# Block 0 of a fused cross-attention and FP4 feed-forward kernel: the ring place in the down weights' room given up for four more bias sums, and the last four pairs of tiles projected in quarters

## What is computed

```
xn   = layernorm(x)
h    = tanh(text_proj[t] + feat_proj[row] + b)     # for every row, every one of 77 tokens, 512 wide
rho  = sum over the 512 of h * w                   # one score for each row and token
att  = softmax over tokens; two gates per row, tanh(att . u) and tanh(att . v)
x    = x + gate_w * xn + gate_b
x    = x + fp4_linear(silu(fp4_linear(xn2, w_gate)) * fp4_linear(xn2, w_up), w_down)
```

## Time and profile before

| | before |
|---|---|
| median of 3 runs | 1538.8 us (1537.33 to 1539.91) |
| the profiled execution's own time | 1539.24 us |
| its span | 1537.4 us |
| busy share of PE, ACT, DVE, POOL | 93%, 88%, 75%, 16% |
| chain that ended last: PE, ACT, DVE | 52%, 27%, 17% |

### The profile page before, as it was taken

The page is one execution under the profiler, slowest core; times in us unless marked ns, Lnnn a source line. Parts: engine busy times, 40 slices in busy tenths (PEclk is TensorE's granted clock), DMA queues, the critical chain, the costliest instruction groups (busy, mean ns, idle before and its releaser), DMA issues.

```text
span 1537.4 us, 24122 instructions
## 1 busy us (share of the span) xinstructions
PE 1432.1 (93%) x9752; PEld 647.7 (42%) x9752; DVE 1157.2 (75%) x1783; ACT 1359.6 (88%) x1249; POOL 248.7 (16%) x389
## 2 busy tenths in 40 slices
PE   7988889856999999999999999989999999999998
PEld 4444444411333333334444444434444444555564
DVE  4699997944586666759666776698877787898887
ACT  5999989999999999999999999999999999433321
POOL 0122222200111010111011111011101111312211
PEclk9999999988999999999999999999999999999999
DMA  5133332320011111201111111112111111123332
GB/s 159 42 83 83 83 82 75 95 65 8 8 26 41 40 27 41 40 15 40 41 40 40 41 33 37 36 40 40 40 41 41 40 41 40 40 59 73 80 69 62
DMA packets 181557, 77.91 MB, mean 51 GB/s; under 512 B 163627, under 2 KB 165675, under 8 KB 181445
## 3 DMA queue, kind: packets, MB, share of 16 engines
q1 hardware_dynamic: 180224, 75.00, 21.0%
q10 hardware_dynamic: 1221, 1.36, 0.3%
HBM read 27.85 MB, written 8.39 MB: 24 GB/s over the span
## 4 chain that ended last, share of the span: by engine, by line
PE 52%; ACT 27%; DVE 17%; issue 2%; DMA 1%; POOL 1%; SPq 0%; ACTq 0%; DVEq 0%; POOLq 0%
PE rho L809 19%; ACT hring L628 17%; PE dn L906 10%; PE gu1g L892 5%; PE gu0g L892 5%; PE gu1u L892 5%; PE gu0u L892 5%; ACT hring L623 4%; DVE featT L985 2%; ACT wd_room L628 2%; DVE work L1019 2%; ACT featT L623 1%; ACT featT L628 1%; DVE work L1040 1%; DVE work L1039 1%
## 5 line engine op out<-in xcount | busy, mean ns | idle before, releaser
L628 ACT ACTIVATE hring<-featT,bias 128x1024 f32<-128x1024 f32 x688 | 729.2, 1156 | 2.6 <-PE rho L809 2.5
L809 PE MATMUL rho<-hring,wslide 128*32 128x512 f32 x3776 | 459.0, 611 | 61.5 <-ACT hring L628 52.4
L809 PEld LDWEIGHTS rho<-hring,wslide 128*32 128x32 f32 x3776 | 105.5, 111 | 338.6 <-issue 191.7
L628 ACT ACTIVATE featT<-featT,bias 128x1024 f32<-128x1024 f32 x220 | 236.3, 1178 | 2.2 <-PE rho L809 2.2
L906 PE MATMUL dn<-wd_room,turned 128*128 128x512 f16 x1023 | 230.6, 380 | 0.2 <-DMA turned<-work 0.2
L490 POOL TENSOR_SCALAR split_t<-sm 128x32 f32<-128x32 f32 (+4 forms) x82 | 19.7, 240 | 1178.1 <-DVE sm L1008 1178.1
L623 ACT ACTIVATE hring<-featT 128x4096 f32<-128x4096 f32 x57 | 207.5, 3640 | 0.4 <-DVE featT L985 0.4
L985 DVE TENSOR_SCALAR featT<-featT,bias 128x1024 f32<-128x1024 f32 x256 | 175.5, 750 | 11.9 <-ACT hring L623 7.6
L1309 DVE TENSOR_TENSOR work<-sg,gu1u 128x352 f32<-128x352 f32 x64 | 33.3, 521 | 173.9 <-ACT sg L661 173.1
L906 PEld LDWEIGHTS dn<-wd_room,turned 128*128 128x128 f16 x1023 | 96.4, 98 | 145.2 <-issue 36.0
L809 PE MATMUL rho<-featT,wslide 128*32 128x512 f32 x1056 | 126.4, 596 | 5.4 <-ACT featT L628 3.1
(11 more groups left out here) (228 smaller groups left out, 1578.5 us busy)
## 6 DMA issues: line engine op xcount, KB each, us to landing
xt<-in_x SPq DMA_DIRECT2D x32, 256.0 KB, 2.8
out<-xt SPq DMA_DIRECT2D x32, 256.0 KB, 2.3
work<-in_x SPq DMA_DIRECT2D x8, 512.0 KB, 4.1
xt<-in_x SPq DMA_DIRECT2D x6, 512.0 KB, 4.3
xt<-in_L_ffn_w_gate SPq DMA_DIRECT2D x11, 256.0 KB, 2.7
xt<-in_L_ffn_w_up SPq DMA_DIRECT2D x11, 256.0 KB, 3.0
work<-in_L_ffn_w_down SPq DMA_DIRECT2D x2, 704.0 KB, 5.1
xt<-in_L_ffn_w_down SPq DMA_DIRECT2D x2, 704.0 KB, 4.1
```

The costliest lines, as they stand in the source:

```text
L628: act.activation(slot[s][:, g, :], featT[:, e, ROW0[k]:ROW0[k] + rows], ACT.Tanh, bias=bias[:, e, base + tok:base + tok + 1]).then_inc(tan ...
L809: last = pe.matmul(rho[SLOTW * g:SLOTW * g + SLOTW, hf * 512:hf * 512 + 512], wslide[:, e, SLOTW - 1 - r:2 * SLOTW - 1 - r], slot[s][:, g, ...
```

## The change

It does three things in block 0.

- The ring has two places from quad 43 to quad 76: place 3 is given up. Its bytes stay the room of the bias sums.
- Four more quads are summed: 49, 53, 58 and 62, twelve in all. Round w = 8 of DVE's list gets two sums (quads 49 and 53), and two more stand behind `copy_pair(10)` (quad 58) and behind `down_weights(0)` (quad 62). SP now starts its transposes into `wd_room` when ACT has finished tanh 62.
- Pairs 8 to 11 (w = 9 to 12) are projected in quarters of 8 profile instructions behind the quads at + 1 to at + 4: 49 to 52, 54 to 57, 58 to 61 and 63 to 66. The transposes of pair 11 come behind the last quarter of pair 9, at quad 57.

```diff
--- before.py
+++ after.py
@@ -69,9 +69,9 @@
 
     assert BLOCKS == (1024,) * 4
     DEPTH = (2, 2, 3, 3)
-    HEAD_PLACE = [4] * 43 + [None] * 2 + [3] * 16 + [None] * (QPB - 61)
-    SUM_ROUNDS = (0, 2, 4, 6)
-    FIRST_SUMS = (13, 17, 22, 26, 31, 35, 40, 44)
+    HEAD_PLACE = [4] * 43 + [None] * (QPB - 43)
+    SUM_ROUNDS = (0, 2, 4, 6, 8)
+    FIRST_SUMS = (13, 17, 22, 26, 31, 35, 40, 44, 49, 53, 58, 62)
     ring_pos, ring_prev = [], []
     last_user = [-1] * 5
     for k in range(NBLK):
@@ -81,7 +81,7 @@
             ring_pos.append(at)
             ring_prev.append(last_user[at] if last_user[at] >= 0 else None)
             last_user[at] = QPB * k + q
-    LAST_IN_WD, LAST_IN_FEATURES = last_user[3:]
+    LAST_IN_FEATURES = last_user[4]
 
     G_COST, D_COST = 3.6, 2.4
     slots = {}
@@ -400,7 +400,7 @@
             sp.wait_ge(pair_turned, PAIRS)
             passed()
             load_wd(1)
-            sp.wait_ge(quad_used, LAST_IN_WD + 1)
+            sp.wait_ge(tanh_ready, GRP * (FIRST_SUMS[-1] + 1))
             for r in range(KC):
                 sp.wait_ge(wdq_ready, r + 1)
                 passed()
@@ -614,10 +614,6 @@
                     act.wait_ge(pair_ready, PAIRS)
                 if s == 2 and ring_prev[n] is None:
                     act.wait_ge(tanh_ready, GRP * n)
-                if s == 3 and ring_prev[n] is None:
-                    act.wait_ge(feat_filled, len(FEAT))
-                    act.wait_ge(text_filled, KC)
-                    act.wait_ge(tanh_ready, GRP * (FIRST_SUMS[-1] + 1))
                 if n in SUMMED:
                     act.wait_ge(summed, GRP * (SUMMED[n] + 1))
                     act.activation(slot[s], rooms[room_of[n]], ACT.Tanh).then_inc(tanh_ready, GRP)
@@ -824,19 +820,19 @@
                         last = pe.transpose((tr, dn)[t][:, k * P:k * P + P], xpair[p % 2][:, t, k * P:k * P + P], idf[:])
                 last.then_inc(pair_turned, 1)
 
-            def project_pair(p, half):
+            def project_pair(p, chunks):
 
                 pe.wait_ge(pair_copied, p + 1)
                 if p < 2:
                     pe.wait_ge(uv_ready, 1)
                 else:
                     pe.wait_ge(pair_ready, p - 1)
-                for e in (2 * half, 2 * half + 1):
+                for e in chunks:
                     for k in range(KC):
-                        last = pe.matmul(gu[p % 2][half][:, (e % 2) * 256:(e % 2) * 256 + 256],
+                        last = pe.matmul(gu[p % 2][e // 2][:, (e % 2) * 256:(e % 2) * 256 + 256],
                                          Wf[:, k, e * P:e * P + P], xnT2[p % 2][:, k, :],
                                          start=(k == 0), stop=(k == KC - 1))
-                if half == 1:
+                if KC - 1 in chunks:
                     last.then_inc(pair_projected, 1)
 
             for n in range(QPB):
@@ -859,10 +855,9 @@
                     at = 8 + 9 * w // 2
                     if n == at and w < PAIRS:
                         turn_pair(w)
-                    if n == at + 1 and w > 0:
-                        project_pair(w - 1, 0)
-                    if n == at + 2 and w > 0:
-                        project_pair(w - 1, 1)
+                    per = 1 if w > 8 else 2
+                    if w > 0 and n > at and per * (n - at) <= KC:
+                        project_pair(w - 1, range(per * (n - at - 1), per * (n - at)))
 
             def softmax_transposes(k, hf):
                 pe.wait_ge(rho_drained, k + 1)
@@ -1203,8 +1198,10 @@
                 if w in SUM_ROUNDS:
                     sum_quad()
             copy_pair(NC - 1)
+            sum_quad()
             features_pair(NC - 2)
             down_weights(0)
+            sum_quad()
             copy_pair(NC)
             features_pair(NC - 1)
             down_weights(1)
```

## The result

| | before | changed kernel |
|---|---|---|
| median of 7 runs each | 1538.99 us | 1543.88 us (1540.86 to 1545.48) |
| ratio | | 1.0029, 95% interval 1.0019 to 1.0039 |
| the profiled execution and its span | 1539.24, 1537.4 | 1540.86, 1539.1 |
| eleven further runs, beside 33 of before | 1538.54 | 1542.52 (1540.79 to 1545.32), ratio 1.0023 (1.0014 to 1.0032) |

The changed kernel is slower, by 0.2 to 0.4%. The forecast of 1541.7 has the sign and the place; the median of the first runs is 2.2 us above it and that of the further ones 0.8, both inside the range. One run of before (1563.72) was a disturbed one and is left out of the ratio.

The account below looks back on a forecast made before the run. ACT was taken to bound block 0: quad 63 starts 3.5 us later, less 0.58 before quad 67, so 2.9 us later; on a median of 1538.8 that gives 1541.7 us, range 1539.5 to 1544.5.

Parts of the forecast that it names:

- ACT sets block 0, and its loss reaches the end at full size: ACT bounds the end of block 0; what it gains or loses before quad 76 reaches the kernel's end undiminished.
- Four fused tanh save 2.64: On ACT, four more fused tanh at 3.50 us against 4.16 save 2.64 us if sums and places are ready.
- Two places: about 1.3 us before quad 49, nothing else: With two ring places quad 49 waits for score 47 and starts at 233.8, not 232.5 us.
- Quarters take the wait before quad 67 away and cost nothing: Quarters on PE fit under ACT's 4.16 us per quad, so the 0.58 us before quad 67 goes; boundaries cost nothing.
- Two sums push the statistics by 5.32, and PE waits 2.9 us for POOL: Sums 49 and 53 delay DVE's statistics 5.32 us; PE waits 2.9 us before turning pair 10, costing ACT nothing itself.
- The sum of quad 62 is 5.0 us late: DVE makes this sum behind `down_weights(0)`, ending at 290.8 us; ACT wants it at 285.9 and stalls 5.0 us.
- the clock, which I took as 0: PE's clock may fall after idling before pair 10's transposes, adding 0 to 1.5 us; 0 was taken.
- rival 2: Late sum of quad 62, and PE's clock falls before score 54: 4.4 us later, 1543.2 us; chance 0.27.
- Rival 3: The sum of quad 62 is in time: quad 76 comes 2.1 us earlier, 1536.7 us; chance 0.08.
- Rival 4: The two-place ring stalls ACT at several quads: 0.5 to 1.5 us on top of 2.9, 1542.7 us; chance 0.1.
- Rival 5: The loss is absorbed later, in the feed-forward: 0 to 1.5 us later, 1539.5 us; chance 0.07.
- The rule on batches: Matmuls should run back to back; by it quarters would cost up to 1.5 us, by the profile rows nothing.

Follow-up runs that it names:

- again: The changed kernel run again without edits, for a second profile and eleven more runs: 1542.52 us, ratio 1.0023.
- sum 62 earlier: The changed kernel with DVE making the sum of quad 62 before `down_weights(0)` and not behind it: 1538.04 us, ratio 0.9991.
- three sums: The changed kernel without its fourth new sum, quad 62 being an ordinary quad: 1538.14 us, ratio 0.9996.
- halves: The changed kernel with pairs 8 to 11 projected in halves as before: 1541.85 us, ratio 1.0019.
- pairs 6, 7 too: The changed kernel with the sum of quad 62 before `down_weights(0)` and pairs 6 and 7 also in quarters: 1537.78 us, ratio 0.9994.
- and without sum 53: The kernel of "pairs 6, 7 too" with the sum of quad 53 also removed: 1537.68 us, ratio 0.9986.
- third place, quarters: The kernel before, keeping its third ring place and eight sums, with pairs 6 to 11 projected in quarters: 1534.49 us, ratio 0.9973.
- again3: The changed kernel profiled once more without edits, the faster of two further looks: 1540.44 us.
- again2: The changed kernel profiled once more without edits, the slower of two further looks: 1544.53 us.

## Why the prediction was right, and by how much

A count of ACT's waits orders the kernels. Take the waits from quad 44 on in the profile, subtract those of before (3.07 + 0.58), and subtract 0.66 for each further fused tanh:

| kernel | waits, us | further sums | sum of both against before | measured medians |
|---|---|---|---|---|
| changed, first profile | 3.07, 0.93, 5.42 | 4 | +3.1 | +4.9; again +4.0 |
| sum 62 earlier | 3.07, 1.29, 1.26 | 4 | -0.7 | -0.5 |
| three sums | 3.07, 1.10, 0.91, 0.22 | 3 | -0.3 | -0.4 |
| halves | 3.07 and 6.04 | 4 | +2.8 | +3.3 |
| quarters alone | 3.07 | 0 | -0.6 | -1.2 |
| two places alone | 3.07 and 3.74 | 0 | +3.2 | +3.0 |
| pairs 6, 7 too | 4.18, 1.18 | 4 | -0.9 | -1.2 |
| and without sum 53 | 4.10 | 3 | -1.5 | -1.3 |
| third place, quarters | none | 0 | -3.7 | -4.3 |

Eight of the nine agree within 0.7 us. The changed kernel itself does not: its medians lie 0.9 to 1.8 above the count. The count is of one profile and the medians are of other executions, and it does not see what happens to the last scores of block 0; both matter below.

**ACT sets block 0, and its loss reaches the end at full size.** Right: 1185.7 us behind the drain against 1185.5, and the table.

**Four fused tanh save 2.64.** Right; 3.50 from start to start again (289.51 to 293.03 is 3.52).

**Two places: about 1.3 us before quad 49, nothing else.** 0.93 to 1.29 over the profiles. Right for the changed kernel. The part alone shows what the quarters spare it: with halves there are four more such waits, 0.58 to 0.94 us each (the 0.58 before quad 67 was there before).

**Quarters take the wait before quad 67 away and cost nothing.** Right, in the whole and alone (0.9996). The wait has gone in every profile with quarters.

**Two sums push the statistics by 5.32, and PE waits 2.9 us for POOL.** 2.67, 2.69 and 2.50; right. In the fourth profile of the changed kernel (run again), whose first 210 us took 1.7 us longer, it was 1.21. The part of the step that this is no cost of its own was right for ACT at full clock only.

**The sum of quad 62 is 5.0 us late.** 5.42 and 5.41 in two profiles, 4.79 in a third, the one in which PE waited only 1.21 for POOL (I had put 4.7 for PE ready at once), 5.68 in the one with the clock down behind the turn of pair 10. Shown by moving that one call: the wait goes and the time with it. The exact time of the wait hangs on how far ACT was ahead: in the first profile quad 49 waited 0.93 and not 1.3, so ACT came to quad 62 0.4 sooner, and stood there 0.4 longer.

**The term that was mis-sized is the clock, which I took as 0.** "I take 0, being nearer the 2.67" picked the smaller of two cases that both occur. The four profiles of the changed kernel, cut at common instructions (us):

| execution | start of quad 44 | quad 44 to 63 | quad 63 to the drain | drain to the end |
|---|---|---|---|---|
| before, 1539.24 | 212.32 | 78.60 | 61.02 | 1185.5 |
| changed, 1540.86 | 210.69 | 82.34 | 60.33 | 1185.7 |
| again3, 1540.44 | 210.91 | 82.33 | 60.33 | 1185.1 |
| again2, 1544.53 | 211.25 | 84.02 | 62.05 | 1185.4 |
| again, 1544.17 | 212.41 | 81.76 | 61.36 | 1186.9 |

Where the clock stayed up at the two places named below, quad 44 to the drain takes 142.67 and 142.66 us against 139.62 before. The change itself costs 3.05 us, and the sum had 2.9. One profile (again2) had the clock down behind the turn of pair 10 (+1.7 us). Two (again2 and again) had it down at the end of block 0, a place that the prediction did not name. In run again the softmax transposes and the last scores ran at half clock there:

```profile
353.00:356.00 3.00, 2.48 (x16) 0.32 (x8) 0.47 (x1) 3.00 (x4) 0.00 (x0) 0.54 0.00 0
356.00:359.00 3.00, 2.04 (x10) 2.07 (x10) 0.81 (x1) 3.00 (x4) 0.00 (x0) 0.50 0.02 5
359.00:362.00 3.00, 3.00 (x16) 1.82 (x19) 2.15 (x5) 1.44 (x3) 0.00 (x0) 0.50 0.00 0
```

Against the first profile run again takes 1.0 us more before the drain and 1.1 behind it. Another 1.7 us of this execution lie ahead of quad 44, in the part that the change leaves as it was. So its time is not the clock at the end of block 0 alone.

The medians, 1542.5 and 1543.9, are 0.8 and 2.2 us above the forecast. That is rival 2 in size (4.4 us later), but only in part by its mechanism, and that the measured 4.9 and 4.0 came so near to it is partly luck: half clock behind the turn of pair 10 was in one of four profiles, and the other losses lay at places that no rival named. Which of the unprofiled runs had full clock can't be told: both profiled executions of the low group also reached quad 44 earliest. The prediction set the term by the one idle stretch of 2.67 us. The later profiles show how little its length says. Over all profiles in which PE waited for POOL before the turn of pair 10, score 54 was slowed to between 3.26 and 3.58 us in five (behind 1.84, 2.21, 2.50, 2.64 and 2.64 us of idling) and not in three (1.21, 2.67, 2.69), so half clock there was at least as likely as 0.

Rival 3, the sum in time, is what the moved call makes of the kernel, 0.5 to 1.4 us faster, and not 2.1, since the clock fell in its profile too (1.26 before quad 56). Rival 4 is what halves would have given. Rival 5 is out: what was lost before the drain was not made up behind it.

**The rule on batches** (the Trainium skill, "Perfetto Trace Analysis", Matmul Optimizations): by it the quarters should have cost something; on the kernel before they did not, 0.9996 (0.9987 to 1.0004). The rule that the moment of a clock change differs from run to run (the Trainium skill, "TensorE: Matmul & The Clock Gate", Part 1) is borne out: the same kernel, 2.50 us of idling with the clock down behind it and 2.67 and 2.69 without.

## What to carry to other kernels

A helper's work that is put at the end of another engine's fixed list costs nothing on that engine and can cost the whole length of what stands before it: follow the list back from the new entry to the last wait in it, and compare with when the consumer arrives. A ring place given up is paid at each burst of its consumer, so shorten the bursts first; here quarters alone were worth 4.3 us once they reached the pair whose halves stood before quad 44, and the place that the change gave up was what covered POOL's late pair. Where a stretch of idling on PE is new and something waits right behind it, count half clock as a likely case and not as a risk; here it came in five of the eight profiles in which PE had waited for POOL before the turn of pair 10. And compare profiles from a common instruction on: the first 210 us of the same program moved by up to 1.9 us.

## What the runs showed of the hardware that was not expected

Idle stretches of PE of nearly the same length before the same instructions left the granted clock at 1.00 (2.67 and 2.69 us) or were followed by less over the next 3 us: 0.55 behind 2.50 us, 0.68 and 0.81 behind 2.64 us, 0.77 behind 2.21 us, and 0.67 behind 1.84 us in one kernel whose earlier rows differ. Length alone does not decide it. The first 210 us of one and the same program also moved by up to 1.9 us between executions (quad 44 at 210.69, 210.91, 211.25, 212.03, 212.32, 212.41 and 212.55), which is as much as most of the effects in the table. In the step from the first profile (210.69) to run again (212.41) most of it goes with the clock: from 180 to 186 us that was 0.50 in run again and 0.72 in the first profile, ACT waited longer for PE behind it, and from quad 35 to quad 41 run again took 1.35 us more. In the profile of before 1.2 us of the difference were there by 80 us, and their cause is open.
